# Cross-attention and a mixture of experts on one core: projections as three rounded products, one context buffer

## What is computed

```python
q = split_heads(layernorm(x) @ wq.T + bq)       # x: (8, 512, 256) float32
k = split_heads(ctx @ wk.T + bk)                # ctx: (8, 512, 256)
v = split_heads(ctx @ wv.T + bv)
attn = softmax(einsum('bhqd,bhkd->bhqk', q, k) / 4)
x = x + merge_heads(einsum('bhqk,bhkd->bhqd', attn, v)) @ wo.T + bo
n = layernorm(x)
gates = top2_normalised(softmax((n @ Wg + bg) / 5))      # 8 experts
x = x + sum_e gates_e * (gelu(n @ W1_e + b1_e) @ W2_e + b2_e)
```

## Time and profile before

| what | value |
|---|---|
| median of 3 runs | 809.06 us (807.59 to 813.81) |
| the profiled execution's own time | 810.81 us |
| its span, first to last instruction | 808.9 us |
| mean granted TensorE clock | 0.992 of full speed |
| PE busy | 757.3 us (94%) |
| DVE busy | 610.6 us (75%) |
| ACT busy | 455.7 us (56%) |
| POOL busy | 394.6 us (49%) |

### The profile page before, as it was taken

How to read it: one execution, slowest core, us unless ns; L and a number is a source line. 1 busy time by engine, 2 the same in 40 slices (tenths; PEclk the granted TensorE clock), 3 DMA queues, 4 the chain that set the end, 5 groups by cost and what they waited for, 6 DMA issues and landing times.

```text
span 808.9 us, 16337 instructions
## 1 busy us (share of the span) xinstructions
PE 757.3 (94%) x4672; PEld 452.5 (56%) x4672; DVE 610.6 (75%) x1126; ACT 455.7 (56%) x663; POOL 394.6 (49%) x357
## 2 busy tenths in 40 slices
PE   9999999999999999999999888769999989999994
PEld 4443344444444444444444333348999879989994
DVE  6787778798798797788787787646777877766773
ACT  2066676775776776766766655843345434444441
POOL 6506143547647637728725603343453555344443
PEclk9999999999999999999999999999999999999998
DMA  6765857757757657757767556876454455454441
GB/s 220 208 180 175 224 169 219 226 170 257 209 177 251 208 191 241 202 178 229 209 176 244 163 160 239 287 266 118 77 94 78 84 129 104 71 78 74 72 70 12
DMA packets 90660, 136.24 MB, mean 168 GB/s; under 512 B 15456, under 2 KB 49216, under 8 KB 90192
## 3 DMA queue, kind: packets, MB, share of 16 engines
q1 hardware_dynamic: 76592, 117.33, 48.1%
q0 software_dynamic: 13296, 17.09, 12.0%
q10 hardware_dynamic: 688, 0.79, 0.3%
HBM read 71.25 MB, written 64.04 MB: 167 GB/s over the span
## 4 chain that ended last, share of the span: by engine, by line
PE 75%; issue 6%; ACT 6%; DVE 5%; DMA 4%; POOL 2%; another core or an unknown queue 0%; SPq 0%; DVEq 0%; POOLq 0%
PE ps_pv L1544 13%; PE ring L1710 10%; PE ring L1692 10%; PE ring L1531 10%; PE ring L1518 7%; PE ps_x L1575 7%; ACT probs L1022 4%; DMA out<-y_sb,xs 4%; PE ps_x L1595 4%; PE ring L1701 3%; PE ps_x L1585 3%; PE ps_x L1605 2%; DVE negm L1094 2%; PE ps_pv L1683 1%; PE ps_x L1562 1%
## 5 line engine op out<-in xcount | busy, mean ns | idle before, releaser
L1094 DVE TENSOR_REDUCE negm<-ring 128x2 f32<-128x1024 f32 x256 | 310.3, 1222 | 75.4 <-PE ring L1518 66.0
L1022 ACT ACTIVATE probs<-ring 128x1024 f32<-128x1024 f32 x256 | 260.2, 1024 | 94.1 <-PE ring L1531 73.0
L910 POOL DMA_INDIRECT out<-y_sb,xs x71 | 110.2, 1553 | 142.8 <-DMA out<-y_sb,xs 87.8
L1544 PE MATMUL ps_pv<-probs,v_aug 128*32 128x512 f32 x1024 | 137.2, 608 | 5.7 <-ACT probs L1022 5.7
L1531 PE MATMUL ring<-kq 64*128 64x512 f32 x512 | 126.2, 492 | 7.3 <-DVE negm L1094 6.1
L1518 PE MATMUL ring<-kq 64*128 64x512 f32 x512 | 106.1, 413 | 10.8 <-ACT probs L1022 6.2
L1531 PEld LDWEIGHTS ring<-kq 64*128 64x128 f32 x512 | 47.5, 183 | 110.5 <-issue 76.2
L1055 ACT CAST xsT_hi<-ps_pv 128x256 fp32r<-128x256 f32 x70 | 26.1, 373 | 132.8 <-PE ps_pv L1683 125.2
L801 POOL DMA_INDIRECT xs_dram<-xg,rows x64 | 63.5, 993 | 55.5 <-DVEq L1262 30.8
L1710 PE MATMUL ring<-w_hi,hT_hi 128*128 x284 | 85.3, 300 | 0.1
L1710 PE MATMUL ring<-w_lo,hT_hi 128*128 x284 | 80.1, 282 | 0.0
(11 more groups left out here) (197 smaller groups left out, 1222.4 us busy)
## 6 DMA issues: line engine op xcount, KB each, us to landing
kq<-k_dram SPq DMA_DIRECT2D x64, 192.0 KB
kq<-q_dram SPq DMA_DIRECT2D x64, 192.0 KB
xs<-xs_dram SPq DMA_DIRECT2D x71, 132.5 KB
k_dram<-qk_hi SPq DMA_DIRECT2D x32, 256.0 KB
q_dram<-qk_hi SPq DMA_DIRECT2D x32, 256.0 KB, 2.7
o_dram<-oT SPq DMA_DIRECT2D x32, 256.0 KB
w_dram<-w_sb SPq DMA_DIRECT2D x12, 512.0 KB
w_hi<-w_dram SPq DMA_DIRECT2D x12, 512.0 KB
```

The lines of the kernel that those rows point to most:

```text
L910: pool.indirect_dma_start(out=out, out_offset=bass.IndirectOffsetOnAxis(ap=xs[j % AHEAD][:, TOKEN:TOKEN + 1].bitcast(I32), axis=0), in_=y_ ...
L1022: nc.scalar.activation(probs[kt][:, 2 * jp:2 * jp + 2, :], ring[PLACE["ST", u, p] % RINGS][:], ACT.Exp).then_inc(exp_done, 1)
L1094: nc.vector.tensor_reduce(negm[:, v % 2, :, jp, kt], ring[PLACE["MX", v, p] % RINGS][:], AX.X, ALU.max, negate=True).then_inc(max_free, 1)
L1544: mm = nc.tensor.matmul(ps_pv[2 * DH * j:2 * DH * (j + 1), :], v_aug[:, kt, HPG * g + j, :], probs[kt][:, j, :], start=(kt == 0), stop=(kt ...
```

## The change

For batches 1 to 7 each float32 product of K, Q and V becomes three fp32r products (batch 0 keeps the float32 ones). This needs high and low parts of the three weights, made once: ACT rounds, POOL subtracts (`low_weights`). The high part of the context is made by ACT in steps (3, 3) and (3, 4) (`high_kv`), the low part by POOL at the end of its list for a stage (`low_kv`), in the place of the context itself. The turned input XT0, XT1 is now read out of `ps_x` twice: ACT writes the high part over `xn`, then DVE subtracts it from the bank (`low_x`, steps (2, 7) and (3, 2)), and only DVE's instruction frees the bank. XT0 moves from step (2, 7) to (2, 6). The context has one buffer, so `load_kv(i + 2)` waits for V1 of batch i + 1 and stands later in SP's list, behind the loads of the experts' weights. Because `xn` now holds the high part, `ln(b)` waits for Q1 of batch b - 1, and POOL's `split("Q", i + 1, 1)` moves ahead of `ln(i + 2)`. The scratch for the descriptors of POOL's transfers is set to 8192 bytes. Two semaphores for biases become one. The core of the diff:

```diff
-NEXT = {(2, 7): "XT0", (3, 1): "XT1"}
+NEXT = {(2, 6): "XT0", (3, 1): "XT1"}
 
 FIRST = {(0, 3): "K0a", (0, 4): "XT0", (0, 5): "K0b", (0, 6): "XT1", (0, 7): "Q0a", (1, 1): "Q0b",
          (1, 3): "Q1", (1, 5): "K1a", (1, 6): "K1b", (2, 3): "V0", (2, 5): "V1"}
+
+XT_LOW = {(2, 7): "XT0", (3, 2): "XT1"}
+
+KV_HIGH = {(3, 3): 0, (3, 4): 1}
 
...
+        wq_hi = sb("wq_hi", [P, DC, D], F32R)
+        wk_hi = sb("wk_hi", [P, DC, D], F32R)
+        wv_hi = sb("wv_hi", [P, DC, D], F32R)
...
-            xn = att("xn", [P, NT, D])
-            xnT = att("xnT", [P, DC, S])
-            kvT = att("kvT", [P, 2, DC, S])
-            wq_sb = att("wq_sb", [P, DC, D])
-            wk_sb = att("wk_sb", [P, DC, D])
-            wv_sb = att("wv_sb", [P, DC, D])
+
+            with ExitStack() as whole:
+                xn = whole.enter_context(nc.sbuf_tensor("xn", [P, NT, D], F32))
+                xnT = whole.enter_context(nc.sbuf_tensor("xnT", [P, DC, S], F32))
+
+                kvT = whole.enter_context(nc.sbuf_tensor("kvT", [P, DC, S], F32))
+                wq_sb = whole.enter_context(nc.sbuf_tensor("wq_sb", [P, DC, D], F32))
+                wk_sb = whole.enter_context(nc.sbuf_tensor("wk_sb", [P, DC, D], F32))
+                wv_sb = whole.enter_context(nc.sbuf_tensor("wv_sb", [P, DC, D], F32))
+            xn_hi = att("xn_hi", [P, NT, D], F32R)
+            xn_lo = att("xn_lo", [P, DC, S], F32R)
+            kv_lo = att("kv_lo", [P, DC, S], F32R)
+            wq_lo = att("wq_lo", [P, DC, D], F32R)
+            wk_lo = att("wk_lo", [P, DC, D], F32R)
+            wv_lo = att("wv_lo", [P, DC, D], F32R)
+            kv_hi = att("kv_hi", [P, DC, S], F32R)
...
             def load_kv(b):
-                if b > 1:
-                    sp.wait_ge(full["V1"], b - 1)
-                sp.dma_start(kvT[:, b % 2], ctx_kv[b]).then_inc(kv_in, 16)
+
+                sp.wait_ge(full["V1"], b)
...
             def body(i):
                 more = i + 1 < B
-                if i + 2 < B:
-                    load_kv(i + 2)
                 if i + 3 < B:
                     load_x(i + 3)
...
                 if i == 0:
                     load_w1(E - 2)
+                if i + 2 < B:
+                    load_kv(i + 2)
                 if more:
                     put_max(i + 1, 0)
...
             load_stack(0, 1)
-            load_kv(1)
             store_parts("Q", 0, 1)
             store_parts("K", 0, 1)
+            load_kv(1)
             put_max(0, 0)
...
-                pool.wait_ge(full["XT1"], b)
+                if b == 1:
+                    pool.wait_ge(full["XT1"], b)
+                else:
+
+                    pool.wait_ge(full["Q1"], b)
                 for t in range(NT):
                     nc.gpsimd.tensor_scalar(xn[:, t, :], x_of(b)[:, t, :], mv[:, t, 0:1], rstd[:, t:t + 1],
                                             ALU.subtract, ALU.mult).then_inc(xn_done, 1)
+
+            def low_weights(n):
+
+                kind = "KQV"[n]
+                whole_w, high, low = w_parts[kind]
+                pool.wait_ge(full[{"K": "K1a", "Q": "Q1", "V": "V1"}[kind]], 1)
+                if kind == "V":
+                    pool.wait_ge(full["V0"], 1)
+
+                pool.wait_ge(w_split, 3)
+                nc.gpsimd.tensor_tensor(low[:], whole_w[:], high[:].bitcast(F32), ALU.subtract).then_inc(w_split, 1)
+
+            def low_kv(b):
+                pool.wait_ge(kv_split, 3 * b - 1)
+                nc.gpsimd.tensor_tensor(kv_lo[:], kvT[:], kv_hi[:].bitcast(F32), ALU.subtract).then_inc(kv_split, 1)
 
...
                     split("Q", i + 1, 0)
+                    split("Q", i + 1, 1)
                 if i + 2 < B:
                     ln(i + 2)
                 if i + 1 < B:
-                    split("Q", i + 1, 1)
                     split("K", i + 1, 1)
...
+                if i + 2 < B:
+                    low_kv(i + 2)
...
+            for n in range(3):
+                low_weights(n)
+            low_kv(1)
...
-                if kind == "XT":
-                    if b > 0:
-                        act.wait_ge(full["Q1"], b)
+                if kind == "XT" and b == 0:
                     nc.scalar.copy(xnT[:, int(name[2]), :], ps[:]).then_inc(done[name], 1)
+                elif kind == "XT":
+
+                    nc.scalar.copy(xn_high(int(name[2])), ps[:].rearrange("p (t s) -> p t s", s=P)).then_inc(xt_high, 1)
                 elif name[0] == "V":
...
+            def high_kv(b, c):
+                act.wait_ge(kv_in, 16 * (b + 1))
+                nc.scalar.copy(kv_hi[:, c, :], kvT[:, c, :]).then_inc(kv_split, 1)
 
...
+                        if i + 2 < B and (g, p) in KV_HIGH:
+                            high_kv(i + 2, KV_HIGH[g, p])
...
+            for kind in "KQV":
+                whole_w, high, _ = w_parts[kind]
+                nc.scalar.copy(high[:], whole_w[:]).then_inc(w_split, 1)
             misc("MT", 0)
+            for c in range(DC):
+                high_kv(1, c)
...
+            def low_x(name, b):
+                c = int(name[2])
+                dve.wait_ge(xt_high, 2 * (b - 1) + c + 1)
+
+                dve.wait_ge(full["Q1"], b)
+                nc.vector.tensor_tensor(xn_lo[:, c, :].rearrange("p (t s) -> p t s", s=P), ps_x[:].rearrange("p (t s) -> p t s", s=P),
+                                        xn_high(c).bitcast(F32), ALU.subtract).then_inc(done[name], 1)
...
+                            if name[:2] == "XT" and b == 1:
+                                low_x(name, b)
+                        if i + 2 < B and (g, p) in XT_LOW:
+                            low_x(XT_LOW[g, p], i + 2)
...
-                    w, act_t = (wq_sb, xnT[:]) if name[0] == "Q" else (wk_sb, kvT[:, b % 2])
+                    w, act_t = (wq_sb, xnT) if name[0] == "Q" else (wk_sb, kvT)
                     half = columns(name, b)
                     ps = claim(name, b)
                     if name[0] == "Q":
                         pe.wait_ge(done["XT0"], b + 1)
                         pe.wait_ge(done["XT1"], b + 1)
+                    elif b == 0:
+                        pe.wait_ge(kv_in, 16)
                     else:
-                        pe.wait_ge(kv_in, 16 * (b + 1))
-                    for c in range(DC):
-                        mm = nc.tensor.matmul(ps[:, half], w[:, c, f * P:(f + 1) * P], act_t[:, c, half],
-                                              start=(c == 0), stop=(c == DC - 1))
+                        pe.wait_ge(kv_split, 3 * b)
+                    if b == 0:
+                        for c in range(DC):
+                            mm = nc.tensor.matmul(ps[:, half], w[:, c, f * P:(f + 1) * P], act_t[:, c, half],
+                                                  start=(c == 0), stop=(c == DC - 1))
+                    else:
+                        pe.wait_ge(w_split, 4 if name[0] == "K" else 5)
+                        _, w_hi, w_lo = w_parts[name[0]]
+                        for c in range(DC):
+                            if name[0] == "Q":
+                                high = xn_high(c)[:, half.start // P:half.stop // P, :]
+                                low = xn_lo[:, c, half].rearrange("p (t s) -> p t s", s=P)
+                                res = ps[:, half].rearrange("p (t s) -> p t s", s=P)
+                            else:
+                                high, low, res = kv_hi[:, c, half], kv_lo[:, c, half], ps[:, half]
+                            for n, (w, src) in enumerate(((w_hi, high), (w_hi, low), (w_lo, high))):
+                                mm = nc.tensor.matmul(res, w[:, c, f * P:(f + 1) * P], src, start=(c == 0 and n == 0),
+                                                      stop=(c == DC - 1 and n == 2))
                     mm.then_inc(full[name], 1)
...
-                    pe.wait_ge(kv_in, 16 * (b + 1))
+                    if b == 0:
+                        pe.wait_ge(kv_in, 16)
+                    else:
+                        pe.wait_ge(kv_split, 3 * b)
+                        pe.wait_ge(w_split, 6)
                     for h in range(2):
-                        for c in range(DC):
-                            t = 2 * n + h
-                            mm = nc.tensor.matmul(ps[:, h * D:(h + 1) * D], kvT[:, b % 2, c, t * P:(t + 1) * P],
-                                                  wv_sb[:, c, :], start=(c == 0), stop=(c == DC - 1))
+                        tokens = slice((2 * n + h) * P, (2 * n + h + 1) * P)
+                        if b == 0:
+                            for c in range(DC):
+                                mm = nc.tensor.matmul(ps[:, h * D:(h + 1) * D], kvT[:, c, tokens],
+                                                      wv_sb[:, c, :], start=(c == 0), stop=(c == DC - 1))
+                        else:
+                            terms = [(x, w, c) for c in range(DC) for x, w in ((kv_hi, wv_hi), (kv_hi, wv_lo), (kv_lo, wv_hi))]
+                            for k, (x, w, c) in enumerate(terms):
```

(23 more changed lines are left out.)

1 line of the change is left out of this document (removed).

## The result

The changed kernel took 839.94 us (median of 4 runs, 837.16 to 841.12) against 808.92 for the kernel before on the same chip: 1.035 times, 95% interval 1.032 to 1.039. Slower by 31 us, where 5 us of gain were forecast and the range ended at 815. The profiled execution took 841.12 us, its span is 839.2 (before 808.9), its mean granted clock 0.967 of full speed (0.992).

What follows compares the result with a forecast made beforehand. PE sets the pace on average, with DVE or ACT last in some steps. Stages 2 to 5 gain 4.0 us, stages 1 and 6 1.1 each, stage 0 loses 1.2: -5.0, from 809.06 to 804.0 us; range 796 to 815.

Steps and rivals of the forecast that it cites:

- Products: K, Q, V products on PE: K0a 0.91, Q1 1.59, V0 and V1 1.62 us each; 1.83 us saved a batch.
- the sign that I had named: In the profile after, PE's busy time down by about 12 us, but the span by 5.
- V's gain and XT0's move: Groups 2 and 3: V's 0.60 us gain all gone, XG0 waits 0.3; together they end 0.15 us later.
- Groups 0 and 1: Cheaper K and Q products and earlier routing on DVE: a stage gains 0.45 us, before the split's part.
- the split's part: Q1's split ahead of `ln`: 0.8 us off the routing, 0.25 given back, gain 0.55 in stages 2 to 5.
- Stage 0: Loses 1.2 us: `low_x` delays, and context issued behind two weight loads, landing after 6.3 us, at 95.9 against 95.4 wanted.
- `low_x` in stage 0: Delays MT and Q0a by 0.4 to 0.8 us, where DVE runs five maxima without a gap.
- Ring: Descriptor scratch at 8192 bytes for POOL's scatters and adds: costed at nothing.
- the fourth rival: Ring too small, XG0 waits some 4 us in six stages: 828 us or more; chance 0.04.
- Rivals: All PE's saving arrives (0.17), DVE bounds (0.14), POOL's scaling holds routing (0.10), ring too small (0.04), projections no cheaper (0.05).
- The second: DVE becomes the bound, MT and XG0 wait 1.2 us each in stages 0 to 5: 818 us; chance 0.14.

Runs made afterwards that it cites:

- b_move: Kernel before with the second split of the queries moved ahead of the normalisation on POOL; 799.75 us, 1.000 of before (800.63).
- a_both_again: Changed kernel with that split back behind the normalisation and the context's load ahead of the expert weights' loads, measured again; 794.72 us, 0.995 of before (800.63).
- a_order: Changed kernel with the second split of the queries put back behind the normalisation; 810.19 us, 0.999 of before (811.3).
- move_2: Kernel before with the second split of the queries moved ahead of the normalisation, once more on another chip; 832.52 us, 1.026 of before (811.82).
- both_2: Changed kernel with split back behind the normalisation and context's load ahead of the expert weights' loads, once more; 804.15 us, 0.989 of before (811.82).
- after_again: Changed kernel as it is, measured again on a chip whose before took 800.63; 806.97 us, 1.008 of before.
- both orders mended: Changed kernel with split back behind the normalisation and context's load ahead of the expert weights' loads; 0.991, 0.995 and 0.989 of before on three chips.
- both7_2: Changed kernel with both orders mended and SCATTER at 7 instead of 5, measured again; 801.88 us, 0.989 of before (809.62).
- b_nopace: Kernel before with its eight scatters of a stage no longer paced by the score units; 832.66 us, 1.029 of before (811.3).
- b_ring: Kernel before with only the descriptor ring set to 8192 bytes; 809.94 us, 0.999 of before (811.3).
- a_both: Changed kernel with split back behind the normalisation and context's load ahead of the expert weights' loads; 793.22 us, 0.991 of before (801.25).

## Why the prediction was wrong

- **Products: right.** 0.90, 1.60 and 1.61 us. What of it reaches the pace is small, as forecast. The third chip shows it best, at a granted clock of 1.00: from `b_move` to `a_both_again` PE's busy time falls from about 60.0 to 58.0 us in each of stages 2 to 5 (753.8 to 740.2 in all), while these stages take 60.5 us on average in both. In the changed kernel of the first measurement the sign that I had named, PE's busy time down by 12 us, did not come (757.3 to 757.1), since the clock was lower after each hold.
- **V's gain and XT0's move: right.** In the changed kernel MX of (3, 0) starts at 154.10 after waiting 0.80 us for ACT, and XG0 waits 0.26 us for `low_x` (0.3 forecast). Without the hold, groups 2 and 3 change by +0.2 us a stage (117.3 against 116.5 for the four stages), forecast 0.15.

```profile
154.10 0.50 PE L1591 MATMUL ring<-kq 64*128 64x512 f32 x2 [0.80 <-ACT probs L1077]
...
159.78 0.66 PE L1635 MATMUL ps_x<-ident,xg 128*128 128x128 f32 x4 [0.26 <-DVE xn_lo L1199]
```

- **Groups 0 and 1: right in kind, the split's part too large.** Forecast for a stage was -1.0 with the split's part, which is -1.15 in these two groups, as the other two were to lose 0.15; stages 2 to 5 of the changed kernel came to -1.0, -0.8, -0.4 and -0.7. The second `row_k`, 1.01 us in the earlier trace rows, took 0.31, 0.45, 0.37 and 1.12 us there: held far less in three stages of four. With the split put back (`a_order`) the groups still gain 0.5 us a stage, so the split is worth about 0.3, not 0.55.
- **The step that failed** is "K1's split comes about 2 us later and the scatter with it; XG0 has some 5 us of slack over `xg`, of which 2 go: nothing". I asked who waits for the scatters' end, and not what the scatters' start is tied to. They come 4.9 us later, not 2, since the moved split waits 7.3 us for Q0's stores: I had it end 19.7 us after stage 4's first exponent (at 305.4), and it ended 23.1 us after it. And a delay past the score units of the pacing removes the pacing. On a chip with the hold that costs 20.7 us by itself (`move_2`). The prediction itself names the 1.27 us spacing; the 1.67 us "remote" wait, in the row just above, which I left out, would have asked the question.
- **Stage 0: mechanism right, size off.** I had the context "behind two weight loads", and took 6.3 us to landing from the earlier trace rows, the median of issues that have no such loads ahead. It was 10.3 us from the issue to ACT's use, and stage 0 lost 6.0 us instead of 1.2; stage 1 lost 1.1 instead of gaining 1.1, at a mean granted clock of 0.96. In the eleven traces of kernels with the new products whose stage 1 ran at 1.00 it took 59.2 to 60.0 us, a gain of 0.2 to 1.0. Issuing the context first gives 5.7 of it back.
- **`low_x` in stage 0: too small a term.** I gave it 0.4 to 0.8 us. MT of the first group waits for it, and it stands behind DVE's statistics, which wait for a load of `x`; before, MT waited for neither. In the thirteen traces of kernels with the new products that wait of MT is 0.7 to 1.8 us, and the first group takes 15.6 to 19.1 us instead of 14.9. It was 1.25 us in the changed kernel, and 1.8 in `both_2`, where the granted clock then was at its lower level (0.50) from 51.8 to 58.6:

```profile
49.02 0.76 DVE L1166 BATCH_NORM_STATS2 stats<-x_all 128x6 f32<-128x256 f32 x2 [1.84 <-DMA x_all<-in_x]
51.56 0.28 PE L1626 MATMUL ps_x<-ident,negm 128*16 128x128 f32 x1 [1.83 <-DVE xn_lo L1199]
```

- **Stage 7, +4.7 us,** which I gave no term: its eight scatters are unpaced in both kernels. Both show a hold of 3.9 us there on ACT, and the changed kernel more around it. On the third chip its groups 0 to 2 took 45.0 us in `after_again` and 44.0 in `b_move`. On the chips with the hold they range from 45.4 to 51.3 us over the kernels with the new products, so part of the 4.7 may be chance. What sets the rest was not tried.
- **Ring: right at no cost,** and the fourth rival is out down to 4096 bytes. I missed that it gains, below.
- **Rivals.** None had this mechanism. The second (DVE late) appears on the third chip only: MT waits 1.18 us for `lg` in stage 3 of `after_again`, whose first groups of stages 3 to 6 take 15.7 to 17.3 us instead of 15.0. Without the hold the changed kernel is at 1.008 of before there: 6.7 us in the last group of stage 0 and 0.6 to 1.8 us a stage of this kind in stages 3 to 5 against the gain.

With both orders mended the total comes near the forecast, but by luck. On a chip like that of the first measurement the mended kernel took 804.15 us against 811.82; forecast were 5.0 us of gain, measured 7.7 by the medians (5 to 13 by the interval). But the forecast put the gain into stages 1 to 6 and nothing behind them. On the third chip the spans of `b_move` and `a_both_again` differ by 4.9 us, of which 4.0 lie behind group 2 of stage 7 and 0.9 before it. Against the profile of before, `both_2` is 6.0 us shorter, of which 4.1 lie there; stages 2 to 5 give 1.6 us together, and stage 0 takes 3.0 back. Of these 4 us at the end 1.6 are the ring's; the rest is not explained, and the same stretch differs by 4.7 us among the five traces of kernels with the old products and the default ring (288.9 to 293.6 us).

## What to carry over

When an instruction is moved on an in-order queue, look up what each later entry is tied to in front as well as behind: a wait that paces a burst works only as long as the burst arrives before it. A landing time taken from the median of all issues is wrong for the one issue that is put behind two large ones. A wait that the profile puts on nobody ("remote") in a kernel with one core is a row to explain before an order is touched. And a total that fits is no proof of a sum: compare it stage by stage.

## What the runs showed of the hardware

- **The hold.** In the first measurement and on three of the five chips of the experiments (before at 809.6 to 811.8 us), ACT and DVE, and POOL where it waited for PE, did not see finished work of PE while an unbroken run of indirect transfers from POOL was in flight, up to 8 us. On the two chips of 801 us no trace showed it, `b_move` and `after_again` with their unbroken runs of eight included. With a spacing of 1.7 us and more (`both7_2`) stages 2 to 6 had none. With 1.27 us the third groups were about 1.3 us longer than without the hold for six and two, or four and four, and 1.6 to 9.7 us longer for eight, 5.7 and more in most stages; that includes the slower clock behind it. Which path carries it is not shown: whether the bytes or the issuing matter was not tried.
- **The ring and the end of the kernel.** POOL's last instruction, which closes the kernel, took 3.71 us in every trace with the default ring (kernels `before`, `b_nopace`, `b_move`, in the first measurement and on three chips), 2.08 in every one with 8192 bytes and 1.01 in the one with 4096. The medians are too coarse to show it: `b_ring` is at 0.995 to 1.002 of before. The 1.6 us are part of the 4.5 us by which the end of the changed kernel is shorter.
- **The clock** followed the stalls: 0.967 granted in the changed kernel, 0.991 in `both_2`, 0.998 in `a_both` on a chip without the hold. Stages 2 to 5 ran at means between 0.92 and 0.98 in the changed kernel, where PE stood for 3.9 to 6.6 us at each hold, and at 1.00 in the kernel before, where it stood for less than 1 us at a time.
